# DLRM tower on one Trainium2 core: weights loaded early, the last half's packs by tile, its last store on two queues, one MLP layer ahead of the last tile's rows

## The reference

```python
e = stack([tbl_f[ids[:, f]] for f in range(27)], axis=1)      # 2048 x 27 x 128
x = einsum('bfd,bgd->bfg', e, e)[:, f > g]                    # 351 pair products
h = concatenate([bottom, x, bottom], axis=1)                  # bottom: 2048 x 128
h = relu(h @ W_top1 + b_top1)                                 # 607 -> 512
h = relu(h @ W_top2 + b_top2)                                 # 512 -> 256
y = h @ W_top3                                                # 256 -> 1
```

## Time and profile before

| what | us |
|---|---|
| median of 3 runs | 378.96 (377.74 to 380.42) |
| the profiled execution's own time | 379.7 |
| its span, first to last instruction | 377.9 |
| mean granted TensorE clock | 0.982 of full |

### The profile page before, as it was taken

The page is one execution under the profiler, slowest core; times in us unless marked ns, Lnnn a source line. Parts: engine busy times, 40 slices in busy tenths (PEclk is TensorE's granted clock), DMA queues, the critical chain, the costliest instruction groups (busy, mean ns, idle before and its releaser), DMA issues.

```text
span 377.9 us, 10285 instructions
## 1 busy us (share of the span) xinstructions
PE 341.6 (90%) x4321; PEld 330.9 (88%) x4321; DVE 248.2 (66%) x332; ACT 145.9 (39%) x280; POOL 263.0 (70%) x283
## 2 busy tenths in 40 slices
PE   0667857979899999999999999999999999999996
PEld 0566657979899999999999999999999999998985
DVE  3689994868459918794669546982879456962051
ACT  1467762262531354134431553135313443146202
POOL 6777777777777777777777777777777777773030
PEclk9979998998999999999999999999999999999999
DMA  7987749233724264435333352435343533322230
GB/s 172 232 200 216 193 113 305 68 90 76 241 79 117 68 193 108 107 80 188 111 89 84 94 201 72 105 74 191 104 104 81 187 112 89 82 63 73 51 29 1
DMA packets 46905, 45.76 MB, mean 121 GB/s; under 512 B 32944, under 2 KB 35782, under 8 KB 46860
## 3 DMA queue, kind: packets, MB, share of 16 engines
q1 hardware_dynamic: 35950, 27.04, 26.9%
q0 software_dynamic: 8896, 17.89, 17.0%
q10 hardware_dynamic: 2014, 0.18, 0.4%
HBM read 39.52 MB, written 5.55 MB: 119 GB/s over the span
## 4 chain that ended last, share of the span: by engine, by line
PE 82%; DVE 6%; DMA 4%; ACT 3%; issue 3%; SPq 1%
PE work L441 41%; PE gram L468 14%; PE work L453 6%; PE work L494 4%; PE work L495 4%; PE work L496 4%; DMA raw_lo<-in_tbl 4%; DVE onehot L601 3%; PE work L511 2%; PE work L513 2%; PE work L512 2%; PE work L522 2%; DVE tab_lo L586 2%; SPq L331 1%; DVE w_lo L611 1%
## 5 line engine op out<-in xcount | busy, mean ns | idle before, releaser
L411 POOL DMA_INDIRECT emb<-in_tbl,ids_all x272 | 259.1, 953 | 84.0 <-issue 80.2
L601 DVE TENSOR_TENSOR onehot<-ids_bc,row_idf 125x1024 fp32r<-125x1024 int32 (+2 forms) x232 | 199.0, 919 | 38.2 <-PE work L441 32.6
L441 PE MATMUL work<-onehot,tab_hi 125*128 125x256 f32 x672 | 172.7, 296 | 24.9 <-ACT tab_hi L707 13.0
L441 PE MATMUL work<-onehot,tab_lo 125*128 125x256 f32 x672 | 168.9, 290 | 2.5 <-issue 2.5
L441 PEld LDWEIGHTS work<-onehot,tab_hi 125*128 125x128 f32 x672 | 133.5, 199 | 33.5 <-issue 18.5
L441 PEld LDWEIGHTS work<-onehot,tab_lo 125*128 125x128 f32 x672 | 133.9, 199 | 0.0
L749 ACT COPY embT<-work 128x512 f32<-128x512 f32 (+1 forms) x36 | 26.8, 797 | 103.3 <-PE work L441 103.3
L468 PE MATMUL gram<-embT 128*54 128x52 f32 x1920 | 51.5, 214 | 2.4 <-ACT embT L571 2.2
L468 PEld LDWEIGHTS gram<-embT 128*54 128x54 f32 x1920 | 49.5, 130 | 4.7 <-issue 1.4
L756 ACT COPY inter<-gram 118x416 f32<-118x416 f32 x64 | 32.4, 507 | 16.7 <-PE gram L468 15.8
L494 PE MATMUL work<-x_hi,w_hi 128*128 128x256 f32 (+1 forms) x128 | 36.9, 288 | 1.8 <-DVE embT L571 0.9
(11 more groups left out here) (55 smaller groups left out, 220.5 us busy)
## 6 DMA issues: line engine op xcount, KB each, us to landing
ids_bc<-in_sel_ids SPq DMA_DIRECT2D x14, 512.0 KB, 4.4
grams<-inter SPq DMA_DIRECT2D x64, 84.5 KB
emb<-in_tbl,ids_all POOLq DMA_INDIRECT x272
ids_bc<-in_sel_ids SPq DMA_DIRECT2D x11, 256.0 KB, 8.6
misc<-in_tbl SPq DMA_DIRECT2D x3, 448.0 KB
inter<-in_tbl SPq DMA_DIRECT2D x3, 448.0 KB
misc<-in_bottom SPq DMA_DIRECT2D x8, 128.0 KB
raw_w<-in_W_top SPq DMA_DIRECT2D x4, 256.0 KB, 7.4
```

Of the source, the lines that this page charges most:

```text
L411: pool.indirect_dma_start(out=emb[:, t % TILE_SLOTS, f, :], out_offset=None, in_=gather_tables[f], in_offset=bass.IndirectOffsetOnAxis(ap= ...
L441: mm = nc.tensor.matmul(out, part[0:k, CHUNK_AT[f] + c, :], onehot[0:k, at % RING, i * HALF:(i + 1) * HALF], start=(c == 0 and i % 2 == 0 ...
L601: nc.vector.tensor_tensor(onehot[0:k, at % RING, 0:width], ids_bc[0:k, four[0]:four[-1] + 1, :].rearrange("p i n -> p (i n)"), row_idf[0:k ...
```

## The change

- **Weights.** `load_weights` goes. SP issues the loads of W_top1's bottom blocks behind the staging of the eighth select table (n = 7), of chunk 2 behind the ninth, of chunk 1 behind the tenth, and of chunk 0 and W_top2 behind the first ids of half 1. ACT rounds all of them right behind the extraction of tile 0, ahead of select_out(1, 0). DVE adds the bottom blocks before one-hot block 5 of half 1; the splits stay before block 13.
- **mlp1(6)** goes ahead of rows(15) on TensorE, with its relu on ACT (line 779, no more on DVE) and its split on DVE ahead of the copies of tile 15's rows.
- **mlp3(6)** goes from behind mlp1(7) to directly behind mlp2(6); DVE does the relu of mlp2(6) (line 639) before it rounds the packs.
- **Last store.** Of tile 15's four store DMAs SP issues two and ACT two.
- **Packs of half 7 by tile.** 28 packs with tile 14's part and 28 with tile 15's, each with half the bytes. Tile 14's: SP issues 7 (EARLY_FIRST) before the last store and 6 (EARLY_SECOND) behind its part of it, ACT 6 behind its part of it, POOL 9 as soon as tile 14 is stored. Tile 15's, once it is stored: SP 12, ACT 12, POOL 4, as before.

```diff
+    EARLY_POOL = PACKS[2::3]
+    EARLY_FIRST, EARLY_SECOND, EARLY_ACT = [[pack for pack in PACKS if pack not in EARLY_POOL][n::3] for n in range(3)]
...
+        def load_packs_of_tile(eng, t, packs, loaded):
+            at = t % 2 * QUADS
+            for f, g, n, c, k in packs:
+                eng.dma_start(packed[k:k + n, c, at * QS:(at + QUADS) * QS].rearrange("k (s n) -> k s n", s=QUADS),
+                              grams[t, :, f, g:g + n, :].rearrange("s k n -> k s n")).then_inc(loaded[c], 16)
...
+                if n >= NSEL - 3:
+                    load_w1(X_ORDER[n - (NSEL - 3)])
...
             def store(t):
                 sp.wait_ge(extracted, (t + 1) * GRAMS)
+                store_quads(sp, t, range(QUADS if t + 1 < TILES else TWO))
+                if t + 1 == TILES:
+                    load_packs_of_tile(sp, t - 1, EARLY_SECOND, packs_loaded)
                 sp.wait_ge(stored, 16 * QUADS * (t + 1))
...
                 load_ids(1, j)
+                if j == 0:
+                    load_w1(X_ORDER[CH])
+                    sp.dma_start(raw_w2[:, 1, :, :], w_top2.rearrange("(c p) n -> p c n", p=P)).then_inc(w2_loaded, 16)
...
-            load_weights()
...
+                if h + 1 == HALVES:
+                    sp.wait_ge(packed_split, CH * h)
+                    load_packs_of_tile(sp, 2 * h, EARLY_FIRST, packs_loaded)
                 store(2 * h + 1)
...
             pool.wait_ge(packed_split, CH * (HALVES - 1))
+            pool.wait_ge(stored, 16 * QUADS * (TILES - 1))
+            load_packs_of_tile(pool, TILES - 2, EARLY_POOL, packs_pool)
             pool.wait_ge(stored, 16 * QUADS * TILES)
-            load_packs(pool, HALVES - 1, POOL_PACKS, packs_pool)
+            load_packs_of_tile(pool, TILES - 1, POOL_PACKS, packs_pool)
...
                 mlp3(h - 2)
+                if h + 1 == HALVES:
+                    mlp1(h - 1)
                 rows(2 * h + 1, range(NGR))
-                if h < HALVES - 1:
+                if h + 1 < HALVES:
                     mlp1(h - 1)
                 products(2 * h + 1, range(GRAMS))
-            mlp1(HALVES - 2)
             mlp1(HALVES - 1, X_ORDER[:1])
             mlp2(HALVES - 2)
+            mlp3(HALVES - 2)
             mlp1(HALVES - 1, X_ORDER[1:])
-            mlp3(HALVES - 2)
...
+                if n == RING:
+                    sum_w1_bottom()
...
+                if h + 1 == HALVES:
+                    split_h1(h - 1)
                 for g in range(1, NGR, 2):
                     rows_out(dve, nc.vector.tensor_copy, 2 * h + 1, g)
-            relu_last()
+            relu2_last()
             split_packed(HALVES - 1)
-            relu2_last()
...
             extract_all(0)
+            for c in X_ORDER:
+                round_w1(c)
+            round_w2()
             select_out(1, 0)
...
+            act.wait_ge(extracted, TILES * GRAMS)
+            store_quads(act, TILES - 1, range(TWO, QUADS))
             act.wait_ge(packed_split, CH * last)
+            load_packs_of_tile(act, TILES - 2, EARLY_ACT, packs_loaded)
             act.wait_ge(stored, 16 * QUADS * TILES)
-            load_packs(act, HALVES - 1, ACT_PACKS, packs_loaded)
+            load_packs_of_tile(act, TILES - 1, ACT_PACKS, packs_loaded)
+            result(last - 1)
             relu1(last)
-            result(last - 1)
```

More of the change, by code:

```diff
@@ L65, in dlrm_tower @@
     SP_PACKS, ACT_PACKS = [[pack for pack in PACKS if pack not in POOL_PACKS][n::2] for n in range(2)]
-    POOL_PACKS_OF = [len([pack for pack in POOL_PACKS if pack[3] == c]) for c in range(CH)]
+    EARLY_POOL = PACKS[2::3]
+    EARLY_FIRST, EARLY_SECOND, EARLY_ACT = [[pack for pack in PACKS if pack not in EARLY_POOL][n::3] for n in range(3)]
+    POOL_PACKS_OF, EARLY_POOL_OF = [[len([pack for pack in packs if pack[3] == c]) for c in range(CH)] for packs in (POOL_PACKS, EARLY_POOL)]
     assert CH == 3
@@ L177, in dlrm_tower @@
         take_mlp(h - 2, "mlp2", "mlp3")
+        if h + 1 == HALVES:
+            take_mlp(h - 1, "mlp1")
         take_rows(2 * h + 1)
         take_gram(2 * h + 1)
-        if h < HALVES - 1:
+        if h + 1 < HALVES:
             take_mlp(h - 1, "mlp1")
-    take_mlp(HALVES - 2, "mlp1")
     claim_mlp1(HALVES - 1)
-    take_mlp(HALVES - 2, "mlp2")
+    take_mlp(HALVES - 2, "mlp2", "mlp3")
     signal_mlp1(HALVES - 1)
-    take_mlp(HALVES - 2, "mlp3")
     take_mlp(HALVES - 1, "mlp2", "mlp3")
@@ L307, in by_tile, with store_quads @@
             return bank(*key)[:, 0:HALF].rearrange("d (s t b) -> d t s b", s=QUADS, t=2)
+        def load_packs_of_tile(eng, t, packs, loaded):
[3 more added lines that the diff above has]
+                              grams[t, :, f, g:g + n, :].rearrange("s k n -> k s n")).then_inc(loaded[c], 16)
+        def store_quads(eng, t, quads):
+            for q in quads:
+                row, col = q // TWO * SIDE + q % TWO * NF, q % TWO * NG
+                eng.dma_start(grams[t, q, 1:NF, :, :], inter[row + 1:row + NF, col:col + NG, :]).then_inc(stored, 16)
         def load_packs(eng, h, packs, loaded):
@@ L318, in _, with load_w1 @@
         def _(sp):
+            def load_w1(c):
+                if c == CH:
+                    sp.dma_start(raw_w1[:, 1, CH, :], w_top1[0:D, :]).then_inc(w1_loaded[CH], 16)
+                    sp.dma_start(raw_w1[:, 0, CH, :], w_top1[D + PAIRS:, :]).then_inc(w1_loaded[CH], 16)
+                else:
+                    sp.dma_start(raw_w1[0:PAIR_ROWS[c], 1, c, :], w_top1[D + c * P:D + c * P + PAIR_ROWS[c], :]).then_inc(w1_loaded[c], 16)
+                if c == CH - 1:
+                    sp.dma_start(raw_w1[ONES:ONES + 1, 1, c, :], b_top1.rearrange("(o n) -> o n", o=1)).then_inc(w1_loaded[c], 16)
             sp.dma_start(ids_all[:, 0:2, :], ids_v[:, 0:2, :]).then_inc(ids_loaded[0], 16)
@@ L339, in load_ids @@
                 sp.dma_start(ids_bc[:, some, :], sel_ids[h][:, some, :].to_broadcast([P, len(four), HALF])).then_inc(ids_bc_loaded[j], 16)
[L341 to L351, removed]
             def store(t):
                 sp.wait_ge(extracted, (t + 1) * GRAMS)
-                for q in range(QUADS):
-                    row, col = q // TWO * SIDE + q % TWO * NF, q % TWO * NG
-                    sp.dma_start(grams[t, q, 1:NF, :, :], inter[row + 1:row + NF, col:col + NG, :]).then_inc(stored, 16)
+                store_quads(sp, t, range(QUADS if t + 1 < TILES else TWO))
+                if t + 1 == TILES:
+                    load_packs_of_tile(sp, t - 1, EARLY_SECOND, packs_loaded)
                 sp.wait_ge(stored, 16 * QUADS * (t + 1))
@@ L384, in _ @@
                     sp.dma_start(bot[:, :, :], bottom_v[2]).then_inc(bot_loaded, 16)
-                if h:
+                if 0 < h < HALVES - 1:
                     sp.wait_ge(packed_split, CH * h)
-                else:
-                    sp.wait_ge(ones_ready, 1)
-                load_packs(sp, h, PACKS if h + 1 < HALVES else SP_PACKS, packs_loaded)
+                elif h == 0:
+                    sp.wait_ge(ones_ready, 1)
+                if h + 1 < HALVES:
+                    load_packs(sp, h, PACKS, packs_loaded)
+                else:
+                    load_packs_of_tile(sp, 2 * h + 1, SP_PACKS, packs_loaded)
             is_freed(sp, "y", 0)
@@ L624, in split_h1 @@
                                                    op0=ALU.max, op1=ALU.subtract).then_inc(freeing("mlp1", h, b), 1)
[L627 to L633, removed]
             def relu2_last():
@@ L820, in _ @@
             rows_all(2)
-            for c in X_ORDER:
-                round_w1(c)
-            round_w2()
             select_out(1, 1)
@@ L845, in _ @@
                 result(h - 2)
+                if h + 1 == HALVES:
+                    relu1(h - 1)
                 rows_even(2 * h + 1)
-                if h < HALVES - 1:
+                if h + 1 < HALVES:
                     relu1(h - 1)
```

13 lines of the change are left out of this document (7 added, 6 removed).

## The result

The changed kernel takes 380.58 us (median of 22 runs), the kernel before 379.05 on the same chip (22 runs): a ratio of 1.0034, 95% interval 1.0021 to 1.0047. On another chip it was 1.0046 (1.0022 to 1.0071). One of the 22 executions of the changed kernel took 654.25 us, 1.7 times as long as the others and without a profile, and the ratio leaves it out. The profiled execution took 381.8 us with a span of 380.0.

What follows compares the result with a forecast made beforehand. TensorE was taken as the bound, with POOL's gathers nearly as full and capping the front gain. The profiled 379.7 + 0.45 (tail) - 0.1 (mlp3(6)) = 380.05, with the median 0.7 below: 379.3 us, range 376.5 to 382.7.

Steps and rivals of the forecast that it cites:

- Both stalls of the front go: TensorE's stops at 60.70 and 82.5 us and the slow clock behind them vanish: 3.6 to 7.6 us gained.
- The gathers cap it: Odd tiles' rows wait for their last gather at POOL's unchanged pace, so not all 7.6 us of front gain is kept.
- I take 2.4: Front gain kept, in us, from tile 13's 2.6 of slack with a gather landing 3.7 after its start.
- The extraction 5.75 later for the reorder: mlp1(6) ahead of tile 15's rows delays the last extraction by its 48 matmuls, 5.75 us; forecast end 357.4.
- the 0.2 for banks: Tile 15's last row groups wait for banks until mlp1(6) is split: +0.2 us, bounds 0 and 1.4.
- The issue phase: In the tail, 18 issues each on SP and ACT at 0.38 us take 6.85, plus 0.5 for long ones.
- the rival in which the pack phase was transfer: Tail packs limited by bytes, not issue: halved from 9.2 to 4.6 us, total 376.95; chance 0.12.
- Landing 1.5: The tail's last pack lands 1.5 us after its issue, chosen between 1.4 and 2.6 because packs are small.
- Its 12 matmuls (1.7 with the restart): The last chunk, ready at 367.85, decides the end of mlp1(7): its matmuls take 1.7 us, ending at 369.55.
- no wait for the last chunk: Sign in the changed profile that the forecast is wrong: TensorE not waiting for the last chunk would mean faster packs.
- mlp3(6) moved, 0.1 gained: In the tail, mlp3(6) behind mlp2(6) fills TensorE's waiting time; behind mlp1(7) its 0.95 us had covered DVE's split.
- The rival with POOL's late packs: POOL's four last packs start late again and land last: 382.3 us, 383.5 with long issues; chance 0.2.

Runs made afterwards that it cites:

- front_only_b: The kernel before with the early weights alone, none of the tail's edits: 378.26 us, ratio 0.9963 to the kernel before.
- after_16_gathers_b: The changed kernel with the last table's gather left out from tile 4 on (12 of 272 gathers): 378.26 us, ratio 0.9964 to the kernel before.
- no_reorder: The changed kernel with mlp1(6) put back behind the last products, its relu on VectorE again: 378.11 us, ratio 0.9949 to the kernel before.
- after_filler_b: The changed kernel with 18 unused matmuls in TensorE's wait behind mlp3(6): ratio to the kernel before 1.0062 (5 runs), 1.0027 when timed once more (12 runs).
- after_again: The changed kernel itself, unaltered, timed and profiled again beside variants on another chip: 381.23 us, ratio 1.0046 to the kernel before.

## Why the prediction came out right, step by step

- **Both stalls of the front go: right.** The gain is 7.4 us at the end of half 1's selection, of 3.6 to 7.6. The first stall went when the weights' transfers left its place, in `front_only_b` too, as the reading of it as traffic had said; by which way the traffic stopped TensorE stays open.
- **The gathers cap it: right, and shown** by the waits, by `front_only_b` and by `after_16_gathers_b`. The size was off: **"I take 2.4"** rested on a landing 3.7 us after the start, a row of another kind of DMA. By `front_only_b` it is 3.06 (3.20 in `no_reorder`). Kept were 3.1 us.
- **The extraction 5.75 later for the reorder: right.** 353.87 - 3.1 + 5.75 = 356.52, measured 356.53; the 0.2 for banks did not appear. Against the forecast of 357.4 this gives 0.9 us.
- **The issue phase: right.** From the extraction to SP's last issue I had 0.1 + 0.75 + 6.85 + 0.5 = 8.2, measured 8.23 (356.53 to 364.76). The 18 average 0.41 (7.44 / 18). The rule of the Trainium skill ("DMA: Bandwidth & Descriptors", "Issuing engines are not separate DMA queues") that issue time is usually small relative to the DMA does not fit these packs: 7.4 us of issue, about 2.5 from the last one to its use. So the rival in which the pack phase was transfer (365.1 for the last chunk) is out with 368.06.
- **Landing 1.5: wrong by 1.0.** The last chunk is taken up 2.55 us behind SP's last issue and 2.35 behind ACT's. I had two rows, the store's (355.49 to 356.99, which is 1.5 and not the 1.4 that I wrote) and the packs' 2.6, and chose the smaller since the packs are small; the row of the same transfer, 2.6, was right.
- **"Its 12 matmuls (1.7 with the restart)": wrong by 1.7,** the step that failed most. From the split's end at 368.06 to 371.43 it is 3.37. With it the path was wrong: the last chunk did not decide. TensorE waited for the first chunk and then went through all 36 matmuls, the first 24 at half clock up to 369.37, 1.3 us after the last chunk was ready. So the sign "no wait for the last chunk" came up, not because the packs were faster but because TensorE was slower. At full clock, as in `after_filler_b`, the landing decides and the same stretch is 1.75 (367.24 to 368.99), the forecast 1.7. I had priced the half clock only in the rival with POOL, behind a wait of over 3 us, though the earlier trace rows had it behind stops of 2.54 and 2.12. The stop in the tail is 2.41, and I had forecast one of 2 to 3 us myself.
- **mlp3(6) moved, 0.1 gained: right** (0.80 for 0.95).
- **The rival with POOL's late packs (0.2): it did not come.** Its last four begin at 359.72, 2.16 behind the last store issue (ACT's, which ends at 357.56), and take 2.72; before, it was 3.96 (355.49 to 359.45). So 1.8 us of it are gone, and POOL ends its issues 2.3 us ahead of SP.

Together, with their hundredths, -0.87 + 0.03 + 1.05 + 1.67 = 1.88 for 371.43 against 369.55; the median was off by 1.3 only, since the profiled execution was 1.2 above it where 0.7 had been taken; in the profile of `after_again` the clock costs 1.3 less. The sum adds up because every term is measured at the last chunk; it is not the path, for with the clock as it was that chunk could have been ready 1.3 us later at no cost. There is some luck in the number: the extraction came 0.9 earlier than forecast and hid a third of the 2.7 by which the end of the tail was off.

The sentence "a change that trades a gain in front for the same loss behind" is borne out in kind: -0.4% for the front by itself, and +0.8% for the tail as the quotient of two runs (by itself it ran only on the slow chip, 1.0118). The loss is twice the gain, not the same.

## To carry to other kernels

When a stall goes, take the pace of every engine over one period before you book the gain: here POOL needed 42.5 us for what TensorE does in 41.0, at a busy share of 70%, and three fifths of the gain went there. The Trainium skill ("GPSIMD Engine Reference", "Key points") calls GpSimd the only option for indirect DMAs, so such a pace is lowered by fewer gathers, not by another queue. Work moved ahead of a wait is free only as far as the wait is long: of the 5.75 us of the layer ahead of the last rows about 1.5 were free, and the other 4.3 delayed everything behind (the extraction ends 12.87 us behind its start in `after_again`, 343.08 to 355.95, and 8.60 behind the start of the rows in `front_only_b`). And a wait of two microseconds ahead of the last matmuls is priced with the half clock behind it.

## What I had not expected of the hardware

- The half clock behind nearly the same stop isn't the same: after 2.41 us the clock was 0.50 for the whole 6.3 us that followed, after 2.43 us (`after_again`) it was back at about 367.6, after 3.4 us, and after 2.23 us (`after_16_gathers_b`) it was 0.50 for 6.1 us. Behind the stops of 1.31 us in `front_only_b` and 1.44 us in `no_reorder` it stayed at 1.00.
- The same program took 1.66 times as long in every execution on one chip, with TensorE idle for no shown reason in the block of many short matmuls, and the ratios of the variants there were not those of the other chips (the front alone 1.0016 and 0.9963).
